# Second cross attention: the transposes of the probabilities as two 64-query halves, issued with the scores

## The reference, cut to what matters

```
q = (layernorm(x) @ w_q) ; k, v = split(context @ w_kv)      # 16 heads of 64
attn = softmax(q @ k.T / 8)                                   # 512 x 512 for each head and batch
out = (attn @ v) @ w_out + b_out ; x = x + tanh(g) * out * tanh(gate)
```

## Time and profile before

| | us |
|---|---|
| median of 3 runs | 2561.95 (2558.16 to 2563.05) |
| the profiled execution | 2568.06 |
| its span in the profile | 2566.4 |
| PE busy / DVE busy / ACT busy | 2326.1 / 1818.8 / 871.8 |

### The profile page before, as it was taken

The page is one execution under the profiler, slowest core; times in us unless marked ns, Lnnn a source line. Parts: engine busy times, 40 slices in busy tenths (PEclk is TensorE's granted clock), DMA queues, the critical chain, the costliest instruction groups (busy, mean ns, idle before and its releaser), DMA issues. The chain is left out here.

```text
span 2566.4 us, 46634 instructions
## 1 busy us (share of the span) xinstructions
PE 2326.1 (91%) x16954; PEld 1639.0 (64%) x17040; DVE 1818.8 (71%) x5138; ACT 871.8 (34%) x2075; POOL 200.1 (8%) x283
## 2 busy tenths in 40 slices
PE   3878788699999999999899999999888999999998
PEld 1555556445575565667555655656568888888887
DVE  4868678597747657654577777776577878787785
ACT  1757477415024023032255555454331111111110
POOL 1523411101011011010000000000000000000000
PEclk7999899899999999999899999999989999999999
DMA  7435323300000000200100000000030000000000
GB/s 189 69 68 88 48 47 47 132 0 1 1 1 1 1 1 1 99 1 1 44 1 1 1 1 1 1 1 1 1 132 1 2 0 8 0 8 0 0 9 9
DMA packets 43513, 65.30 MB, mean 25 GB/s; under 512 B 5056, under 2 KB 36160, under 8 KB 42688
## 3 DMA queue, kind: packets, MB, share of 16 engines
q1 hardware_dynamic: 43328, 62.88, 10.5%
HBM read 54.48 MB, written 8.39 MB: 24 GB/s over the span
## 5 line engine op out<-in xcount | busy, mean ns | idle before, releaser
L2089 PEld LDWEIGHTS banks<-work,big 128*128 128x128 f32 x2048 | 251.4, 195 | 9.5 <-issue 1.9
L2089 PE MATMUL banks<-work,big 128*128 128x128 f32 x2048 | 253.3, 278 | 1.7 <-ACT work L2180 1.5
L1358 PE MATMUL banks<-big,work 128*128 128x256 f32 x1024 | 242.1, 381 | 0.8
L1788 ACT ACTIVATE work<-banks,work 128x512 f32<-128x512 f32 x256 | 175.2, 691 | 171.5 <-DVE work L1877 171.4
L1260 PE MATMUL banks<-big,work 128*128 128x512 f32 x512 | 224.7, 600 | 4.4 <-DVE work L1481 4.4
L2196 ACT ACTIVATE work<-banks 128x512 f32<-128x512 f32 x128 | 76.4, 597 | 437.2 <-PE banks L2089 437.2
L1358 PEld LDWEIGHTS banks<-big,work 128*128 128x128 f32 x1024 | 195.6, 191 | 37.6 <-issue 0.3
L771 PE MATMUL banks<-ident,work 128*128 128x128 f32 x1024 | 166.0, 287 | 53.4 <-ACT work L888 43.9
L888 ACT ACTIVATE work<-work 128x512 f32<-128x512 f32 x256 | 182.9, 716 | 88.2 <-DVE work L1026 88.2
L1877 DVE TENSOR_REDUCE work<-banks 128x2 f32<-128x1024 f32 x128 | 150.5, 1218 | 82.5 <-PE banks L1683 82.3
L1026 DVE CUSTOM_DVE_ANT_0 work<-banks,big 128x512 f32<-128x512 f32 x256 | 173.4, 686 | 47.8 <-issue 41.2
(11 more groups left out here) (207 smaller groups left out, 4119.6 us busy)
## 6 DMA issues: line engine op xcount, KB each, us to landing
wc<-parts SPq DMA_DIRECT2D x128, 128.0 KB, 6.9
parts<-big SPq DMA_DIRECT2D x16, 384.0 KB, 2.5
big<-in_bias SPq DMA_DIRECT2D x4, 1024.0 KB, 10.5
big<-in_B_val SPq DMA_DIRECT2D x8, 512.0 KB, 6.7
big<-in_B_out SPq DMA_DIRECT2D x1, 4096.0 KB, 20.1
big<-in_D_downT SPq DMA_DIRECT2D x1, 4096.0 KB, 12.8
big<-in_D_up SPq DMA_DIRECT2D x1, 4096.0 KB, 22.2
wc<-in_ctxT SPq DMA_DIRECT2D x1, 2048.0 KB, 7.5
```

What stands on the lines that cost most here:

```text
L1358: last = eng.matmul(XB[qt][:, 0:D], spread[:, w % NG, qt * P:(qt + 1) * P], w_out[:, w, :], start=(w == 0), stop=(w == GE - 1))
L1788: eng.activation(prob[:, n % NS * PAIR + j, :], SB[n % 2][:, j, :], ACT.Exp, bias=low[:, n % NS, j:j + 1], accum_out=rowsum[:, n % NS, j:j ...
L2089: last = eng.matmul(HP[n % 2][:, q * P:(q + 1) * P], down[:, kc * ELO + n * NJ + q, :], xnT[par][:, kc, :], start=(kc == 0), stop=(kc == K ...
```

## The change

`turn_probs` issues two transposes where one stood: 64 queries each, the first from partitions 0 to 63 into TB[0], the second from partitions 64 to 127 into TB[1]. A bank now holds both heads of 64 queries, and both semaphore counts of a query tile are raised at its end. The layout of pT changes with it (eight blocks of 512 instead of two by four), the copies write 64 columns in each of eight blocks, and ScalarE copies the first half of the queries and VectorE the second. The order changes on three engines: PE goes transposes n - 2, scores n, transposes n - 1, scores n + 1, and only then keys, values, projection, queries and weigh; ScalarE makes both copies of a burst ahead of its exponentials; VectorE copies, takes the maximum, copies, takes the maximum.

```diff
-    pT = carve(m, "big2")(2 * PAIR, QT, S)
+    pT = carve(m, "big2")(2 * PAIR * QT, S)
...
+    CW, HALF = 512, P // 2
...
                     for j in range(PAIR):
                         for kt in range(QT):
-                            last = eng.transpose(TB[j][:, kt * P:(kt + 1) * P],
-                                                 prob[:, n % NS * PAIR + j, kt * P:(kt + 1) * P], ident[:, :])
-                        last.then_inc(t_made.sem, 1)
+                            for half in range(2):
+                                r, at = slice(half * HALF, (half + 1) * HALF), (j * QT + kt) * HALF
+                                last = eng.transpose(TB[half][:, at:at + HALF],
+                                                     prob[r, n % NS * PAIR + j, kt * P:(kt + 1) * P], ident[r, r])
+                                if j == PAIR - 1 and kt == QT - 1:
+                                    last.then_inc(t_made.sem, 1)
...
                 for b, t, u, n in bursts():
-                    scores(b, t, u, n)
-                    if n >= 2:
-                        turn_probs(n - 2)
+                    for i in range(2):
+                        if n >= 2:
+                            turn_probs(n - 2 + i)
+                        scores(b, t, u, n, i)
...
-                    if n >= 2:
-                        turn_probs(n - 1)
                     if u == 0 and after[0] < B:
                         queries(*after)
...
-                    eng.activation(pT[:, tile % 2 * PAIR, :, qt * P:(qt + 1) * P],
-                                   TB[0].rearrange("p (k q) -> p k q", q=P), ACT.Copy).then_inc(pt0_ready.sem, 1)
+                    eng.activation(pT[:, tile % 2 * PAIR * QT:(tile % 2 + 1) * PAIR * QT, qt * P:qt * P + HALF],
+                                   TB[0].rearrange("p (k q) -> p k q", q=HALF), ACT.Copy).then_inc(pt0_ready.sem, 1)
...
-                    spread_probs(n, 0)
                     if n >= 2:
                         take_probs(n - 2)
+                        take_probs(n - 1)
+                    spread_probs(n, 0)
...
-                    lowest(n)
-                    lowest(n + 1)
-                    if n >= 2:
-                        take_probs(n - 2)
+                    for i in range(2):
+                        if n >= 2:
+                            take_probs(n - 2 + i)
+                        lowest(n + i)
```

More of the change, by code:

```diff
@@ L1582, in c_attention @@
     low, rowsum, rinv = take(NS, PAIR), take(NS, PAIR), take(NS, PAIR)
-    CW = 512
+    CW, HALF = 512, P // 2
     with ExitStack() as ctx:
@@ L1669, in values, with scores @@
                     last.then_inc(v_made.sem, 1)
-                def scores(b, t, u, n):
-                    if u == 0:
+                def scores(b, t, u, n, i):
+                    if u == 0 and i == 0:
                         eng.wait_ge(k_ready.sem, k_ready.at(b, t + 1))
                         eng.wait_ge(q_ready.sem, q_ready.at(b, t + 1))
[L1676 to L1685, removed]
+                    if n + i >= 2:
+                        eng.wait_ge(p_ready.sem, p_ready.at(0, 2 * (n + i - 1)))
+                    qt = 2 * u + i
+                    for c in range(2):
+                        for j in range(PAIR):
+                            r = slice(j * DK, (j + 1) * DK)
+                            last = eng.matmul(SB[i][:, j, c * 256:(c + 1) * 256], qT[r, t % 2, qt * P:(qt + 1) * P],
+                                              kT[r, t % 2, c * 256:(c + 1) * 256], start=True, stop=True)
+                    last.then_inc(s_made.sem, 1)
                 def turn_probs(n):
@@ L1707, in weigh @@
                             last = eng.matmul(FB[0][j * DK:(j + 1) * DK, :], vtok[:, kt, h * DK:(h + 1) * DK],
-                                              pT[:, t % 2 * PAIR + j, kt, :], start=(kt == 0), stop=(kt == QT - 1))
+                                              pT[:, (t % 2 * PAIR + j) * QT + kt, :], start=(kt == 0), stop=(kt == QT - 1))
                     last.then_inc(av_made.sem, 1)
@@ L1836, in _ @@
                             take_values(b, 0, QT - 1, FB[0])
-                    if n >= 2:
-                        take_probs(n - 1)
                     spread_probs(n + 1, 1)
@@ L1894, in take_probs @@
                         eng.wait_ge(av_made.sem, av_made.at(0, tile - 1))
-                    eng.tensor_copy(pT[:, tile % 2 * PAIR + 1, :, qt * P:(qt + 1) * P],
-                                    TB[1].rearrange("p (k q) -> p k q", q=P)).then_inc(pt1_ready.sem, 1)
+                    eng.tensor_copy(pT[:, tile % 2 * PAIR * QT:(tile % 2 + 1) * PAIR * QT, qt * P + HALF:(qt + 1) * P],
+                                    TB[1].rearrange("p (k q) -> p k q", q=HALF)).then_inc(pt1_ready.sem, 1)
                 def update(b, qt, bank):
```

## The result

The changed kernel takes 2571.03 us in the median of 12 runs (2560.89 to 2580.98), the kernel before 2562.56 in 12, one of which, at 3732.16 us, was slow and is left out of the ratio. The ratio is 1.0037, 95% interval 1.0020 to 1.0053, so 5 to 14 us slower. 2567 was forecast, in 2548 to 2600.

What follows compares the result with a forecast made beforehand. PE was taken to bound the stage (busy 581.5 of 601.5 us). Half transposes' 46 us saving was offset by waits, sum 0 to +1; with clock +4, total +5: median 2567 us, range 2548 to 2600.

Steps and rivals of the forecast that it cites:

- Part 1: Half transposes on PE: a pair in 0.058 us, scores behind lose 0.05; saves 1.43 us a tile, 46 for 32.
- Rival B: Half transposes load one after the other or as long as scores' loads: pair about 0.109 us, 2594; chance 0.15.
- Part 2: Changes of PE's array split: each 0.09 us and an unhidden load; five a tile before and after, counted as zero.
- Rival C: A split change costs nothing for half transposes: 0.4 us less a tile, -13 us, 2550; chance 0.25.
- Part 3: PE's waits in a plain tile, walked step by step: up from 0.53 to 1.95 us, period 16.86.
- (c): PE's wait before second transposes of u = 1, behind VectorE's queries copy, normalisation and transposes copy: 0.95 us.
- (d): PE's wait ahead of weigh for the copy of the values: 0.8 us; gone in tiles with projection.
- The sum: Stage total over plain, projection, norm and last tiles: 0 to +1 us, before the clock.
- D: Rival: PE's clock falls after most long waits, 14 x 1.5 = +20 us, 2583; chance 0.17.
- A: The forecast itself: PE's saving is handed back as waits behind copies, 2558 to 2576 us; chance 0.40.
- The clock: PE's clock falling after some 14 waits of 1.3 to 2.0 us in the stage: 0 to +24, taken as +4.

Runs made afterwards that it cites:

- the old order: Changed kernel's half transposes, but PE, ScalarE and VectorE in the order of the kernel before: 2547.08 us, ratio 0.9938 to before.
- the norm late: Changed kernel, but in bursts u = 1 VectorE makes its part of the next batch's norm behind the two maxima: 2552.56 us, ratio 0.9962 to before.

## Why the prediction was right, step by step

**Part 1** held. A pair takes 0.062 us, not 0.058, in a stretch where two loads and two matmuls go by in each pair; the scores behind them lose the expected 0.05 (0.272 us between their first two matmuls instead of 0.216). Rival B is refuted by the group's 0.55 us. With it falls, for these loads, the rule of the Trainium skill ("TensorE: Matmul & The Clock Gate", section "LDWEIGHTS (loading the stationary operand)"), by which a load of 128 columns takes 107 ns: each row half here goes from one such load to the next in 0.062 us.

**Part 2** held in the count and the price: 0.306 us from the last scores to keys, with 0.216 of work, is the same 0.09 as before. Rival C's free exit doesn't exist, and the old order, with three changes more, is faster all the same.

**Part 3.** Against the walk from the first transposes: second transposes at 1.62 (1.46 forecast), keys 3.18 (3.03), transposes of u = 1 6.94 (6.74), their second 9.34 (9.06), weigh 13.59 (13.28), period 17.18 (16.86). The waits are those forecast in place, cause and size: (c) 0.93 (0.95), (d) 0.72 (0.79). The 0.32 missed arises where work was under-counted: half (0.16) by the first hand-over, as a copy starts 0.75 to 0.78 after the transposes instead of 0.66 (the pair's pace, the group's first load that the walk left out, and a later completion). Another 0.05 has come by the transposes of u = 1: keys are copied 2.02 us after their start (1523.10 to 1525.12), not 1.92, and from there VectorE works almost without a gap up to the copy in (c), so it reaches the copy of the queries 0.25 late; 0.08 is added at (c), and 0.03 or 0.04 behind it. So 17.18 lies outside the 16.7 to 17.0 that the prediction named as its sign of being right, and t = 2 and 3 with norm and projection, 22.06 and 22.25, just outside 20.5 to 22; the mechanism stands, the sizes of the hand-overs were too small.

**The sum.** Tile by tile: plain +0.23 (forecast -0.1), twelve of them +2.8; batch 3 with projection 0.0 (-1.5 for four); batches 1 and 2 with norm +0.9, +1.9, +2.0, +0.7, +11 in all (+9); batch 0 with its start +4.8 (+2); the end of batch 3 -7.8 (-8). Together +10.9, forecast +1. About 1.5 us of it is clock in batch 0; most of the rest is the 0.32 per tile. Two slips of the prediction change nothing here: B, D and half of A make a chance of 0.55 for slower, not 0.47, and work less 1.43 with waits up by 1.42 would leave 16.94, where its walk has 16.86.

**The clock** was forecast at +4 and is the second mis-sized term. It fell three times in the stage against twice before. The one that is new came after PE had stood 1.97 us:

```profile
1304.06 1.12 PE L1696 MATMUL banks<-ident,work 64*128 64x64 f32 x16 [1.97 <-DVE big L1895]
1304.94 2.05 PE L1682 MATMUL banks<-work 64*128 64x256 f32 x8
1306.92 2.23 PE L1667 MATMUL banks<-big,wc 128*128 128x512 f32 x4
```

```profile
1303.00:1308.00 5.00, 3.94 (x26) 2.81 (x27) 3.65 (x5) 1.94 (x5) 0.00 (x0) 0.66 0.00 0
```

Scores took 2.05 instead of 1.11. But in batches 1 and 2 two further waits just as long and six of 1.4 to 1.8 us left it at 2.4 GHz, so rival D fell, and +1 to +2 was right. The length of a wait doesn't decide it: with the norm late, waits of 2.35 and 2.43 us at the start and at the end of the stage left the clock up, where waits of 2.35 and 2.43 us at the same places went with a fall in the changed kernel. What does decide it is open. The total of +5 came near the measured +9 (+10.9 in the stage) because work and waits were 8 too low and the clock 2 to 3 too high: that the two misses went against each other is luck.

## What to carry to other kernels

Here a float32 transpose was paced by its 128 moving columns (0.109 us) with a load of 0.058 hidden beneath; two halves in the two row halves, issued alternately, took 0.062. Count the changes of the array's split with it, at 0.09 us and an unhidden first load each: next to scores, which share the split, the halves gained 0.44 us a group, between whole-array matmuls nothing.

There is one pair of banks, so the next transposes wait for the copy of those before. Keep other PE work between two groups, or PE waits for that copy and for whatever stands ahead of it on its engine. Walk one period with each engine's list in order; what to move is then read off (here a copy that nobody needed yet, and a norm).

## What the hardware showed that was not expected

Sixteen half transposes, eight for each row half in sequence, overlap in part: the second half's first load starts 0.31 us into the group, and the scores' first matmul in one half starts 0.06 us before the other half's third-last transpose. So in this group the starts did not follow the order of the program from one row half to the other; how far ahead one can get was not tried.
